# A graph network's dense-edge scatters cut into four node-ordered segments, the last 108 of 508 moved from the setup into layer 1, behind which 75 dense blocks stand ahead of the pairs

## The reference

```
h = max(layernorm(x), 0)
# network 0, three layers on h
msg = relu(x[src]) + 1e-7
out = softmax_aggregate(msg, dst) + x        # softmax over the edges of a node, per feature
h = relu(batchnorm(out @ W1 + b1)) @ W2 + b2 ; x = relu(h)
# network 1, three layers, with edge attributes
e = relu(ea @ ew.T); agg = segment_sum(e, dst); ...
```

## Time and profile before

| | us |
|---|---|
| median of 3 runs (range) | 4170.22 (4170.03 to 4172.24) |
| the profiled execution's own time | 4165.19 |
| its span, first to last instruction | 4163.4 |
| setup | 0 to 863 |
| layer 1, edge phase | 863 to about 1430 |
| granted TensorE clock, mean of the span | 0.894 |

### The profile page before, as it was taken

How to read it: one execution, slowest core, us unless ns; L and a number is a source line. 1 busy time by engine, 2 the same in 40 slices (tenths; PEclk the granted TensorE clock), 3 DMA queues, 4 the chain that set the end, 5 groups by cost and what they waited for, 6 DMA issues and landing times.

```text
span 4163.4 us, 70803 instructions
## 1 busy us (share of the span) xinstructions
PE 3299.3 (79%) x19961; PEld 2595.9 (62%) x19961; DVE 2217.1 (53%) x5689; ACT 1941.5 (47%) x3697; POOL 2373.3 (57%) x2488
## 2 busy tenths in 40 slices
PE   2287777769898789888699888758788888888887
PEld 0144444458777677777577777746666666666665
DVE  6144333325444555445665445736666666666666
ACT  0222111146555576555585555734444444444444
POOL 2666666646666366666356665255565565565552
PEclk6588988889999899999899999879999999998988
DMA  7155433467777367777367776554444444444442
GB/s 291 54 184 191 138 119 120 124 202 246 248 235 236 117 231 234 251 234 242 110 230 243 243 235 197 151 160 126 124 129 129 127 128 128 128 125 127 127 125 63
DMA packets 419116, 713.14 MB, mean 171 GB/s; under 512 B 75585, under 2 KB 259067, under 8 KB 416098
## 3 DMA queue, kind: packets, MB, share of 16 engines
q0 software_dynamic: 130688, 321.08, 26.0%
q1 hardware_dynamic: 270119, 323.45, 25.5%
q10 hardware_dynamic: 18107, 66.24, 4.2%
HBM read 561.11 MB, written 149.39 MB: 171 GB/s over the span
## 4 chain that ended last, share of the span: by engine, by line
PE 36%; another core or an unknown queue 18%; issue 14%; DVE 14%; ACT 10%; DVEq 2%; ACTq 2%; DMA 1%; SPq 1%; POOL 0%; POOLq 0%
PE ps L1570 17%; PE ps L1593 4%; ACT casts L1466 2%; PE ps L718 2%; DVE acc L2369 2%; DVE acc L2403 2%; PE ps L2242 2%; DVE onehot L2396 1%; PE ps L2221 1%; ACTq L934 1%; DVE acc L2396 1%; PE ps L712 1%; ACT two_parts L1456 1%; PE ps L700 1%
## 5 line engine op out<-in xcount | busy, mean ns | idle before, releaser
L2211 POOL DMA_INDIRECT ring<-h_table,idx_ring x832 | 815.9, 981 | 563.2 <-issue 272.9
L652 POOL DMA_INDIRECT pair_rings<-split_table,src_idx x728 | 713.6, 980 | 409.8 <-issue 202.5
L1570 PE MATMUL ps<-casts,two_parts 128*128 128x500 f32 (+1 forms) x3464 | 823.1, 391 | 141.4 <-DVE two_parts L1660 73.8
L1570 PEld LDWEIGHTS ps<-casts,two_parts 128*128 128x128 f32 x3464 | 646.3, 198 | 280.2 <-DVE two_parts L1660 83.5
L665 POOL DMA_INDIRECT adjacency<-acc x508 | 495.8, 976 | 344.4 <-issue 144.7
L1660 DVE TENSOR_TENSOR two_parts<-work,two_parts 128x512 fp32r<-128x512 f32 (+1 forms) x276 | 187.4, 679 | 588.9 <-ACT two_parts L1456 349.8
L1466 ACT ACTIVATE casts<-spare 128x1000 fp32r<-128x1000 fp8e4 (+1 forms) x471 | 458.9, 974 | 8.5 <-PE ps L1570 4.8
L2308 ACT ACTIVATE work<-acc,vecs 128x512 f32<-128x512 f32 x208 | 150.2, 722 | 562.4 <-DVE acc L2369 303.5
L1456 ACT ACTIVATE two_parts<-work 128x512 fp32r<-128x512 f32 (+1 forms) x276 | 169.7, 615 | 452.8 <-remote 232.5
L2221 PE MATMUL ps<-ident,ring 128*128 128x128 f32 x1664 | 292.3, 298 | 83.6 <-issue 59.2
L2260 PEld LDWEIGHTS ps<-mats,work 128*128 128x128 f32 x1664 | 238.2, 204 | 141.7 <-issue 140.4
(11 more groups left out here) (333 smaller groups left out, 6242.6 us busy)
## 6 DMA issues: line engine op xcount, KB each, us to landing
spare<-adjacency SPq DMA_DIRECT2D x216, 250.0 KB
acc<-e_few SPq DMA_DIRECT2D x208, 256.0 KB
work<-msg_table SPq DMA_DIRECT2D x144, 256.0 KB
work<-in_edge_attr SPq DMA_DIRECT2D x104, 256.0 KB
e_few<-spare SPq DMA_DIRECT2D x52, 512.0 KB
spare<-rel_rows SPq DMA_DIRECT2D x208, 84.0 KB
spare<-adjacency SPq DMA_DIRECT2D x72, 187.5 KB
e_few<-work SPq DMA_DIRECT2D x26, 512.0 KB
```

Of the source, the lines that this page charges most:

```text
L652: e.indirect_dma_start(out=to, out_offset=None, in_=table, in_offset=bass.IndirectOffsetOnAxis(ap=src_idx[:, 2 * i + h, j:j + 1], axis=0)) ...
L1570: ins = e.matmul(bank, parts_of(d)[:, b % 2, q, kind * D:(kind + 1) * D], cast_counts[n % CASTS][:, at:at + width], start=opens, stop=(b = ...
L2211: e.indirect_dma_start(out=rows[:, s, j, :], out_offset=None, in_=h_table, in_offset=bass.IndirectOffsetOnAxis(ap=idx_ring[:, s, j:j + 1], ...
```

## The change

The edges of the dense nodes are laid out anew: each partition's 508 columns are four segments of 127 (`WIDE`), and segment s of all partitions together is the s-th quarter of the edges in node order, so the early columns write only the first regions. This lets the scatters be split in time. The first 400 (`EARLY`) stay in the setup, with the same waits for `few_e0`. The other 108 are the first thing that POOL does in layer 1, ahead of its 336 gathers, and wait for nothing but their own 32-deep ring. Addresses and counts get tiles of their own, since the later phase would overwrite `acc`. DVE's address work runs on four segments, with a few instructions more.

In the setup ACT's queue clears regions 0 and 1 (6 DMAs), loads x, and then clears the rest. POOL's first scatter waits for the first six alone, scatter 127 for the rest.

In layer 1 `step_of` gives the first 75 blocks the steps -15 to -1, five each, ahead of pair 0; the other 121 are spread evenly over the 42 pairs. SP waits for all scatters before it loads counts of region 2. Layers 2 and 3 keep their order.

```diff
+SEGMENTS = 4
+WIDE = COLS // SEGMENTS
+REACH = WIDE + 2 * NEAR
+EARLY = 400
...
+LEAD = 15
+LEAD_BLOCKS = 75
...
+def step_of(layer, n):
 
     r, b = divmod(n, BLOCKS)
+    columns = [sum(widths) for _, widths in REGIONS]
+    before = sum(BLOCKS * w for w in columns[0:r]) + b * columns[r]
+    if layer == 0:
+        lead = sum(columns[k // BLOCKS] for k in range(LEAD_BLOCKS))
+        if n < LEAD_BLOCKS:
+            return n * LEAD // LEAD_BLOCKS - LEAD
+        return (before - lead) * PAIRS // (BLOCKS * sum(columns) - lead)
...
-        def scatters(e, S):
-            e.wait_ge(S("zero_fill"), 16 * FILLS * len(REGIONS))
-            e.wait_ge(S("addresses"), 1)
-            for i in range(COLS):
+        def scatters(e, S, first, end):
+            for i in range(first, end):
                 n = i // EACH
+                if i == 0:
+                    e.wait_ge(S("zero_fill"), 16 * FILLS * 2)
+                if i == WIDE:
+                    e.wait_ge(S("zero_fill_rest"), 16 * (FILLS * (len(REGIONS) - 2) + 1))
                 if i % EACH == 0 and n >= SCATTERS:
                     e.wait_ge(S(f"gather_spread{n % SCATTERS}"), 16 * EACH * (n // SCATTERS))
-                if i % EACH == 0:
+                if i % EACH == 0 and i < EARLY:
                     reached(e, S("few_e0"), 2 * pairs_behind(n))
...
             def pool(e, S):
                 setup_pool(e, S)
                 if again:
                     return
-                scatters(e, S)
-                scattered(e, S)
+                e.wait_ge(S("addresses"), 1)
+                scatters(e, S, 0, EARLY)
+                scattered(e, S, EARLY)
                 split_stored0(e, S)
...
+                    if ready and d == 2 * DUOS:
+                        scattered(e, S, COLS)
...
             def pool(e, S):
+                if ready:
+                    scatters(e, S, EARLY, COLS)
                 for i in range(PAIRS):
...
-                for i in range(PAIRS + 3):
-                    blocks = [n for n in range(ALL_BLOCKS) if step_of(n) == i]
+                for i in range(-lead, PAIRS + 3):
+                    blocks = [n for n in range(ALL_BLOCKS) if step_of(layer, n) == i]
```

More of the change, by code:

```diff
@@ L83, in chunks_before, with blocks_halfway @@
     return sum(len(widths) for _, widths in REGIONS[0:r])
-def step_of(n):
+def step_of(layer, n):
     r, b = divmod(n, BLOCKS)
+    columns = [sum(widths) for _, widths in REGIONS]
[5 more added lines that the diff above has]
+        return (before - lead) * PAIRS // (BLOCKS * sum(columns) - lead)
     if r == 0:
         return b * FIRST_STEPS // BLOCKS
[L91 to L98, removed]
+    first = BLOCKS * columns[0]
+    return FIRST_STEPS + (before - first) * (PAIRS - FIRST_STEPS) // (BLOCKS * sum(columns) - first)
+def blocks_halfway(layer, i):
+    steps = [step_of(layer, n) for n in range(BLOCKS * len(REGIONS))]
     return sum(s < i for s in steps) + sum(s == i for s in steps) // 2 if i in steps else 0
@@ L140, in dense_jobs @@
             for n in range(width // CH):
-                jobs.append((step_of(BLOCKS * (r + 1) - 1) + 3, CUT + at + n * CH, chunks, False))
+                jobs.append((step_of(layer, BLOCKS * (r + 1) - 1) + 3, CUT + at + n * CH, chunks, False))
             at += width
-    out, now = [], -1
+    out, now = [], -LEAD - 1
     for ready, node, least, sparse in sorted(jobs):
@@ L147, in dense_jobs @@
     return out
-JOBS = [j for j in dense_jobs() if j[0] < PAIRS - 1]
-LATE = [j for j in dense_jobs() if j[0] >= PAIRS - 1]
+JOBS_OF = [[j for j in dense_jobs(layer) if j[0] < PAIRS - 1] for layer in range(L)]
+LATE = [j for j in dense_jobs(0) if j[0] >= PAIRS - 1]
 FIRST_OF_LAST = CHUNKS - len(REGIONS[-1][1]) + 1
@@ L922, in act, with clear @@
             def act(e, S):
+                def clear(r):
+                    width = PITCH if sum(REGIONS[r][1]) > PITCH // 8 * 7 else sum(REGIONS[r][1])
+                    rows = adjacency[r * SPAN * PITCH:r * SPAN * PITCH + NR * PITCH, :].rearrange("(p b d) o -> p b (d o)", b=BLOCKS, d=PITCH)
+                    for h in range(FILLS):
+                        at = slice(h * BLOCKS // FILLS, (h + 1) * BLOCKS // FILLS)
+                        n = at.stop - at.start
+                        zeros = Z0[:, 0:-(-n * width // 4)].bitcast(U8)[:, 0:n * width].rearrange("p (b d) -> p b d", d=width)
+                        e.dma_start(rows[:, at, 0:width], zeros).then_inc(S("zero_fill" if r < 2 else "zero_fill_rest"), 16)
                 if not again:
@@ L938, in act @@
                     by_sixteens(e, x_rows[:, at, :], a["x"][:, k * PART * D:(k + 1) * PART * D].rearrange("p (t d) -> p t d", d=D), S(f"x{k}"))
+                if not again:
+                    for r in range(2, len(REGIONS)):
+                        clear(r)
+                    e.dma_start(msg_table[N:NR, :], Z0[0:NR - N, 0:D]).then_inc(S("zero_fill_rest"), 16)
                 row_roots(e, S)
@@ L1295, in edges_phase @@
             columns = iota_w[:, :]
+            lead = LEAD if ready else 0
+            JOBS = JOBS_OF[layer]
             by_node = [work[0:WW, b, 0:2 * D] for b in range(2)]
@@ L1341, in duos_at @@
             def duos_at(i):
-                return [d for d in range(ALL_DUOS) if step_of(first_block(d)) == i + 1]
+                return [d for d in range(ALL_DUOS) if step_of(layer, first_block(d)) == i + 1]
             def blocks_of(u):
@@ L1355, in evacuated @@
             def evacuated(i):
-                return [r for r in range(len(REGIONS)) if step_of(BLOCKS * (r + 1) - 1) + 1 == i]
+                return [r for r in range(len(REGIONS)) if step_of(layer, BLOCKS * (r + 1) - 1) + 1 == i]
             def jobs_of(i):
@@ L1496, in nodes_of_pair @@
                     e.activation(by_node[k % 2], ps[k % 2][0:WW, 0:2 * D], ACT.Copy).then_inc(S("by_node"), 1)
-                for i in range(-1, PAIRS + 3):
+                for i in range(-lead - 1, PAIRS + 3):
                     if len(REGIONS) - 1 in evacuated(i):
```

104 lines of the change are left out of this document (53 added, 51 removed).

## The result

| | before | after |
|---|---|---|
| median (range, runs), us | 4171.2 (4170.0 to 4201.7, 4) | 4317.7 (4307.3 to 4330.2, 4) |
| ratio, 95% interval | | 1.033, 1.028 to 1.039 |
| the profiled execution's own time, its span, us | 4165.2, 4163.4 | 4307.3, 4305.6 |
| first scatter | 73.8 | 53.6 |
| layer 1 begins (POOL's first transfer of it) | 863.5 | 786.3 |

The kernel became 3.3% slower, 146 us, where 71 were forecast; the time lies above the range. The three stretches add up: -77 in the setup, +223 in layer 1, -4 behind it, +142 between the two spans.

The account below looks back on a forecast made before the run. PE was taken to lead without being full, its releases delayed by POOL's unbroken indirect transfers. Setup -65 (start -15, end -50) and layer 1 +136 (210 + 455 against 529) gave +71: 4241 us, range 4150 to 4310.

Parts of the forecast that it names:

- The direction and the mechanism: Whole kernel: slower by 71 us, because unbroken indirect transfers by POOL make PE's releases reach other engines late.
- recorded reading: During POOL's unbroken indirect transfers PE's releases arrive late and PE itself is soon slowed; a pause lets them through.
- The start of the setup: Loading x before half the clears removes ACT's idle before its first square root: -15 us; earlier scatters win nothing.
- The end of the setup: Last 29 pairs run without scatters, at 4.31 us instead of 6.03: -50 us, more excluded.
- Rival C: Setup's slow pairs are not caused by scatters, so its end gains nothing: +121, 4291 us; chance 0.08.
- The lead: Start of layer 1 to POOL's fifth gather, which waits for 72 blocks: 210 us, ends 163 and 241.
- Both readings: Blocks beside layer 1's scatters at 5.84 us (lead ends at 226) or 2.8 us (194); middle 210 taken.
- The gathers behind it: Layer 1's remaining 332 gathers at 1.37 us each, 455 us, the middle between 1.263 and 1.478.
- recorded argument: Gathers in layer 1: less PE work holds POOL up less, but fewer waits mean longer runs and held releases return.
- The sum: Layer 1 +136 and setup -65 give +71 us: 4236 profiled, 4241 as median.
- Rival F: PE not held in the lead and gathers unbroken: layer 1 582 us, total -12, 4158 us; chance 0.26.
- H: Rival: PE held at once, gathers at 1.478 us: layer 1 732 us, total +138, 4308 us; chance 0.08.

Follow-up runs that it names:

- e6: Kernel before with only the early loads of x, split clears and four segments; all scatters in the setup, old block order: 4152.6 us against 4173.1, ratio 0.994.
- e2: Kernel after, but in layer 1 POOL waits before each eighth scatter for PE's progress: 3531.7 us, on a chip where before takes 3569.7, ratio 0.989.
- r_before: Kernel before, unchanged, run again for a trace on the chip of the second round of experiments: 4171.9 us.
- e1: Kernel after with the 108 scatters of layer 1 left out: 3528.2 us, on a chip where before takes 3569.7, ratio 0.988.
- e3: Kernel after with all 508 scatters kept in the setup and 75 blocks still ahead of the pairs: 4253.8 us against before's 4173.1, ratio 1.019.
- e4: Kernel after with 4 matmuls instead of 8 in each early block of layer 1: 3526.5 us, on a chip where before takes 3569.7, ratio 0.988.
- e5: Kernel after with two small writes of zeros by POOL after each eighth scatter of layer 1: 3527.6 us, where before takes 3569.7, ratio 0.989.
- the four experiments on the first: The runs e1, e2, e4 and e5, made together on the chip where before takes 3569.7 us: 3526.5 to 3531.7 us.

## Why the prediction was wrong

**The direction and the mechanism held.** Unbroken transfers of POOL hold back PE's releases, and after is slower by it. The second half of the recorded reading, that PE itself is soon slowed, had little part in the lead: the 16 matmuls at 893.28 took 5.76 us of a period of 44.8.

**The start of the setup: right in size, not in its reason.** Forecast -15; e6 shows the layer beginning 17 us earlier. But the square root moved only from 88.88 to 83.54, since ACT, which issues the second half of the clears behind x, came to its table load at 82.25, not at 72.25:

```profile
27.31 49.10 ACTq L952 DMA_DIRECT2D adjacency<-Z  x6
...
82.25 1.28 ACT L532 ACT_TABLE_LOAD   x1 [82.25 <-issue]
83.54 0.24 ACT L532 ACTIVATE sc<-sc 125x50 f32<-125x50 f32 x1
```

ACT thus gives 5 us. The rest goes with the first scatter, 20 us earlier (53.6, had 73.8), of which I had said that it wins nothing. The first 84 scatters wait for no pair and are one unbroken run, and beside it the normalisation of x is held as in the earlier trace rows. In the kernel before this run ends at 181.8 and the last evacuation of xT comes at 190.9; in the kernel after at 161.5 and 173.0; where nothing is held (e2) the last one comes at 118.4. In e6 the last scatter left 18.5 us earlier than in r_before (826.0, 844.5). That the earlier scatters are the cause was not tried apart.

**The end of the setup: right in its reason, 10 us too low.** Forecast -50; e6 to after is 846.2 to 786.3, -60, though more than 50 was said to be excluded. The price of an undisturbed pair was right; the held ones cost more than the 6.03 us of the earlier trace rows: in e6 the 27 pairs behind the 400th scatter took 170.5 us, 6.3 each, and in the kernel after 114.3. Behind the last of the 400 scatters, at 660.6, the pairs take 4.31 us and DVE's line waits on PE by name instead of "remote":

```profile
706.89 0.69 DVE L839 TENSOR_SCALAR ring<-ps 128x512 f32<-128x512 f32 x1 [1.55 <-PE ps L718]
...
711.30 0.69 DVE L839 TENSOR_SCALAR ring<-ps 128x512 f32<-128x512 f32 x1 [1.77 <-PE ps L718]
...
715.52 0.69 DVE L839 TENSOR_SCALAR ring<-ps 128x512 f32<-128x512 f32 x1 [1.26 <-PE ps L718]
...
719.83 0.69 DVE L839 TENSOR_SCALAR ring<-ps 128x512 f32<-128x512 f32 x1 [1.52 <-PE ps L718]
```

Rival C, that the slow pairs are not the scatters' doing, falls with these rows.

**The lead: the step that failed.** This is what I had for the blocks beside the scatters: "at 5.84 us a block 16 more, so 27" or "2.8 us a block: 33 more, 44 in all". Measured: 12 blocks by the end of the scatters, 22.4 us a block once the hold had begun, and a lead of 268 us instead of 210, also above my upper end of 241. Both readings took a true row for the wrong quantity. The 0.73 us of the earlier trace rows is how far matmuls stood apart in a short hold at the end of a run of gathers; in the lead 16 of them took 5.76 us, 0.36 each. The 11.2 us of the earlier trace rows I took as the time of one release, whatever is in it. But it belonged to four transposes, so it was 2.8 us each, and two blocks of 16 matmuls had to wait 44.8 us. Both numbers stood in the rows. With 2.8 us a matmul the lead can be worked out: 8 blocks until the hold is felt, then two in each 44.8 us, the next two at 938.1, which is 151.8 us into the layer; 60 blocks at 1.82 us from there are 109 more, 261 of the 268.

**The gathers behind it: too low.** Forecast 1.37 us each, 455; measured 484, 1.46, near the upper bound of 1.478. e1 shows 1.30 where nothing is held, e3 1.46 without any scatter in the layer. My argument that PE has less to do then was right and did not help: after the lead POOL issues gathers in long runs (16 in a row in e3 from 1003.92 on, and 2.97 us "remote" behind them), and beside these PE's releases come late again: ACT's L1530 waits 127 us "remote" in the kernel after, none in e1. If a run ends where POOL stands for more than 1 us, 33 of the 38 runs of the kernel before have 8 gathers, and 16 of the 21 behind the lead of the kernel after have 16 or 24; of POOL's 57 us of such waits there, 36 are "remote". In e1 all 332 are one run and nothing is held. The other side of the recorded argument, that fewer waits mean longer runs and held releases come back, is thus what the trace shows. That the runs' length is the cause was not tried apart.

**The sum.** Of the miss 58 us are the lead's, 29 the gathers', -12 the setup's and -4 what follows layer 1: 71, which is the 142 between the spans less the 71 that were forecast. Rival F, by which nothing is held, is what runs e1, e2, e4 and e5 show for close relatives of after, at 1.1 to 1.2% faster; for the chip that gave the result it is wrong. H had the right ingredients at too low a price. What I did not ask is what the lead costs when nothing is held in it: POOL must issue 336 gathers at 1.26, 423 us, and it can't make up for some 155 us at the fifth: with a lead of 160 the gathers may take (529 + 77 - 160)/332 = 1.34 us each, if the setup's 77 are not to be lost. The 1.30 of e1 meets this, the 1.46 of e3 does not.

The Trainium skill ("SBUF — State Buffer", Who interferes with whom) has PE free of interference from other engines. On the chip of e1 the traces agree with it (no "remote" wait, and blocks every 1.82 us beside e5's scatters); on the others PE's releases took 2.8 us a matmul. The page speaks of ports and not of releases, and no run here shows by what path they are held.

**Open:** what differs between the chips, or between the times at which they were used, since each chip was used at one time only; whether a held matmul is itself late or only its signal, since the profile models the ends of matmuls; what path the held releases share with POOL's transfers, and the result of the kernel after where before takes 3570 us.

## What to carry to other kernels

When a wait is "remote" and its time repeats exactly, divide it by the number of instructions behind the release before taking it for a fixed latency, and try the law on a second place of the trace. Ask of the buffers which release the waiting instruction needs: it need not be that of the last work done. Where releases are held so, an engine that issues indirect transfers should not do so in long unbroken runs beside another that works in small released steps: a rest of about 3 us in each 13, or a wait on the other's progress, cost less here than it gave back, though it didn't bring the kernel below before. Work that is moved ahead of a loop whose issuing engine is nearly full takes that engine's time, even where the two use different engines.

## What the runs showed of the hardware

Beside unbroken indirect scatters the releases of PE's matmuls came in order, one matmul's worth in 2.8 us: 11.2 us for 4, 22.4 for 8, 44.8 for 16, with 125 or 500 columns. In the kernel after the hold is seen in ACT's waits some 40 us after the first scatter of the run (786.3 to about 828); it was put off by rests of 0.8 us, and with rests of 2.9 us no engine had a "remote" wait. It outlived the run: in the kernel after POOL stopped at 930.8 and the held rises of `dense` came at 942.96. The matmuls took 0.24 us each before it (16 in 3.90 at 826.72) and 0.36 in it (16 in 5.76 at 893.28), at a granted clock of 0.63; from 855 to 893, where PE stood idle, it was 0.52. Over the whole of the scatters the granted clock was 0.60, with PE busy for 29 of 136 us (windows of L1604 alone):

```profile
790.00:926.00 136.00, 28.85 (x96) 22.38 (x96) 0.60 0.16 41
926.00:1100.00 174.00, 143.82 (x602) 115.04 (x603) 0.94 0.46 139
```

The kernel before took 3568 to 3572 us on one chip and 4165 to 4192 us on three others (4170 to 4202 where the result was measured); the four experiments on the first show no remote wait in the whole trace.
